# The last scatters of a part's rows moved from the attention stage's program into the expert stage's, in both layers of a two-layer transformer

## The reference

```python
x = layernorm(x + attention0(x))        # 16 heads of 8, 2048 tokens of 128, rotary, not causal
x = layernorm(x + moe0(x))              # 8 experts, top 2 of them, d_ff 384, and a shared expert of 128
x = layernorm(x + attention1(x))        # 8 heads of 128, causal, batches of 256 tokens
x = layernorm(x + block1(x))            # x + attn (16 heads of 8, causal, convolution in front), then x + moe1
# moe1: 4 experts, top 1, d_ff 512, no shared expert
#   h = layernorm(x) ; e = argmax(h @ router_w) ; y = (silu(h @ gate_e) * (h @ up_e)) @ down_e
```

## Time and profile before

| | |
|---|---|
| median of 3 runs | 1990.08 us (1985.74 to 1990.87) |
| the profiled execution | 1991.82 us, its span 1990.1 us |
| PE busy | 1785.9 us (90%) |
| DVE, ACT, POOL busy | 1562.2, 1375.0, 438.0 us |
| first layer's expert stage | from 703.4 us |
| second layer's expert stage | from 1891.3 us to the end |

### The profile page before, as it was taken

One profiled execution on the slowest core, in us unless ns is written; L12 is line 12 of the kernel. 1 busy time (PEld: TensorE's weight loads), 2 busy tenths in 40 slices (PEclk: granted clock), 3 DMA queues, 4 the chain that ended last, 5 costly groups with the idle time before them and its releaser, 6 DMA issues. The chain is left out here.

```text
span 1990.1 us, 40762 instructions
## 1 busy us (share of the span) xinstructions
PE 1785.9 (90%) x15944; PEld 978.8 (49%) x15944; DVE 1562.2 (78%) x2305; ACT 1375.0 (69%) x2571; POOL 438.0 (22%) x672
## 2 busy tenths in 40 slices
PE   6799999999999988858899999999679999999786
PEld 2122222222222368846789988989412322233386
DVE  5899999999999443456888888888578979786435
ACT  3499999999999843335566566666347898888432
POOL 4201000000000426323341221221320111122433
PEclk8589999999999988978999999999867999999688
DMA  6000000000000068700000000000100000000175
GB/s 175 1 3 4 4 11 3 3 12 3 4 12 5 20 228 271 258 28 1 1 1 1 1 1 1 1 1 1 56 1 2 5 3 12 5 12 6 44 247 199
DMA packets 50863, 82.01 MB, mean 41 GB/s; under 512 B 9424, under 2 KB 35280, under 8 KB 50544
## 3 DMA queue, kind: packets, MB, share of 16 engines
q1 hardware_dynamic: 44864, 69.53, 11.1%
q0 software_dynamic: 3712, 7.71, 1.1%
q10 hardware_dynamic: 2096, 2.17, 0.4%
HBM read 64.38 MB, written 12.25 MB: 39 GB/s over the span
## 5 line engine op out<-in xcount | busy, mean ns | idle before, releaser
L833 DVE TENSOR_REDUCE a_mx<-psum 128x2 f32<-128x1024 f32 (+2 forms) x832 | 906.4, 1159 | 76.5 <-PE psum L608 43.0
L759 ACT ACTIVATE a_cs<-psum 128x512 f32<-128x512 f32 (+3 forms) x1664 | 856.9, 571 | 80.9 <-PE psum L626 62.7
L649 PE MATMUL psum<-a_cs,a_V 128*16 128x256 f32 (+1 forms) x6400 | 501.7, 384 | 20.8 <-ACT a_OD L739 9.7
L608 PE MATMUL psum<-a_KS,a_QS 48*128 48x512 bf16 (+3 forms) x1664 | 329.9, 388 | 30.6 <-DVE a_mx L833 28.3
L626 PE MATMUL psum<-a_QS,a_KS 51*128 51x512 bf16 (+3 forms) x1664 | 336.8, 379 | 4.9 <-ACT a_cs L759 3.0
L626 PEld LDWEIGHTS psum<-a_QS,a_KS 51*128 51x128 bf16 x1664 | 87.8, 93 | 354.9 <-ACT a_cs L759 310.3
L2231 PEld LDWEIGHTS psum<-b_VW,b_ST 128*128 128x128 f32 x2176 | 247.4, 192 | 2.5 <-DVE X L2363 0.2
L2231 PE MATMUL psum<-b_VW,b_ST 128*128 128x129 f32 x2176 | 248.0, 275 | 0.0
L649 PEld LDWEIGHTS psum<-a_cs,a_V 128*16 128x16 f32 x6400 | 107.2, 94 | 245.1 <-issue 120.6
L2338 DVE TENSOR_TENSOR b_M<-b_M,b_ST 128x512 f32<-128x512 f32 (+3 forms) x264 | 158.0, 599 | 38.1 <-ACT b_ST L2270 7.8
L2270 ACT ACTIVATE b_ST<-psum 128x512 f32<-128x512 f32 (+1 forms) x320 | 149.9, 552 | 41.8 <-PE psum L2213 37.1
(11 more groups left out here) (250 smaller groups left out, 1839.6 us busy)
## 6 DMA issues: line engine op xcount, KB each, us to landing
e_W<-in_l_experts SPq DMA_DIRECT2D x45, 576.0 KB, 5.0
e_W<-in_l_experts SPq DMA_DIRECT2D x21, 768.0 KB, 6.0
e_G<-yg SPq DMA_DIRECT2D x12, 256.0 KB, 4.6
xg<-zeros SPq DMA_DIRECT2D x2, 1518.0 KB, 13.0
a_cs<-in_rope ACTq DMA_DIRECT2D x4, 512.0 KB, 10.1
a_QS<-a_mrow SPq DMA_DIRECT2D x128, 3.0 KB
a_cs<-in_rope SPq DMA_DIRECT2D x1, 2048.0 KB, 7.8
a_num<-a_OD SPq DMA_DIRECT2D x120, 16.0 KB
```

What stands on the lines that cost most here:

```text
L608: mm = pe.matmul(ps[:, 2 * slot + half, 0:width], QS[rows, 2 * p + i, q_cols(qb, qt * P, P)], KS[rows, 2 * p + i, c * BLK:c * BLK + width] ...
L649: mm = pe.matmul(ps[32 * j:32 * j + 2 * HD, AV_BANK, a:b], V[:, kt, HPP * p + j, :], probs(e, a, b), start=(kt == 0 and half == 0), stop=last,
L759: act.activation(probs(HPP * s + j, c, BLK), ps[:, plan.bank(entry), c:BLK], ACT.Exp, scale=scale).then_inc(exp_done, 1)
L833: dve.tensor_reduce(mx[:, pk % 2, qt, 2 * i:2 * i + 2, c], banks, AX.X, ALU.max).then_inc(max_done, 1)
```

## The change

`scatter` gets a range of tiles. The call at the end of the attention stage does the tiles before `AT_END`, and a new call in the expert stage, behind the powers of the late blocks and ahead of the first `give_back`, does the rest. `AT_END` is 5 in the first layer and 2 in the second. `sent[0]` is waited for as before.

```diff
@@ small_head_stage, gpsimd
                 for n in front.early:
                     front.keep_early(pool, n)
-                front.scatter(pool, 0)
+                front.scatter(pool, 0, 0, front.AT_END)
@@ Front.__init__
+            self.AT_END = 5
         else:
...
+            self.AT_END = 2
@@ Front
-    def scatter(self, pool, b):
+    def scatter(self, pool, b, first=0, last=None):
         pool.wait_ge(self.pos_ready, b + 1)
         if b == 0:
             pool.wait_ge(self.half_set, 2)
             pool.wait_ge(*self.blank)
-        for t in self.plan.tiles[b]:
+        for t in self.plan.tiles[b][first:last]:
             for k in range(self.K):
@@ expert_layer, gpsimd
                 following.begin(pool)
                 for n in front.late:
                     front.power(pool, n)
+                front.scatter(pool, 0, front.AT_END)
```

## The result

The changed kernel takes 2000.34 us (median of 5 runs, 1998.93 to 2003.88), the kernel before 1990.08 us (5 runs, 1984.48 to 1990.87). The ratio over all runs is 1.0064, with a 95% interval of 1.0045 to 1.0084, so the change costs 0.64%, about 12.7 us (8.9 to 16.7). This ratio is not the quotient of the two medians, which differ by 10.3 us. It is slower, as forecast, but the forecast was 19.8 us and its range began at 2003.5. The profiled execution took 2000.34 us with a span of 1998.6 us.

What follows compares the result with a forecast made beforehand. Both borders were taken to wait for POOL's scatters, with PE the chain behind. First layer 5.0 plus second 14.8, the borders' gain included, gave 19.8 us on 1990.1: 2010 us, range 2003.5 to 2015.5.

Steps and rivals of the forecast that it cites:

- the order of what is queued behind the scatters: SP's weight loads for tiles 1 to 5 stand behind the row loads; on PE everything behind `turn(0)` waits in order.
- the mechanism in both layers: Expert stages: moved scatters make SP issue rows 14.6 us later; PE waits at `turn(0)` in the second, tile 1 in the first.
- a second part that takes nothing back: Tile 1's delay reaches each stage's end in full, since later row waits (4.32, 4.87 us) are timed by scatters following tiles.
- clock term: First layer, tiles 1 and 2 after PE's wait: the lower clock makes five steps take 6.85 us instead of 5.50, 1.35 more.
- lock between DVE and POOL: DVE's normalizing groups beside moved scatters: at most 0.2 us per layer, left out; the skill's rule would add some 2 us.
- The step that failed: the border: Both borders before the expert stages come 0.78 and 1.89 us earlier, 2.67 us in all, with DVE next in line.
- the weights in the first layer: First layer, tile 1: weights queued behind rows start it 10.5 us after the row issue, +3.7 us (+1.7 to +4.2).
- The term of the first layer: First layer's expert stage: late weights at tile 1, +3.7 us, and lower clock, 1.35 us; sum +5.0 us (1.7 to 5.6).
- The second layer's term: Second layer's expert stage: late rows hold PE 15 us at `turn(0)`, tile 1 14.6 us late, 0.2 for clock; +14.8 us.
- (a): First layer: weights come in time because DMA engines were idle, tile 1 loses nothing; sum +13.8, 2004 us; chance 0.10.
- (b): Both layers: the lower clock lasts longer after PE stands, or DVE blocks scatters about a microsecond; 2014.5 us; chance 0.12.
- (c): Expert stage hides the six scatters completely, only the borders' gain is left: 1987.4 us; chance 0.01.

## Why the prediction was wrong in size

**Right.** What bounds the borders, that the gain there is small against the loss, the order of what is queued behind the scatters, and the mechanism in both layers: rows 15.6 and 16.5 us into the stages (15.4 and 16.5 forecast), PE standing 14.95 us in the second (15), 3.63 us at tile 1 in the first (3 to 5), a second part that takes nothing back, and a clock term of 6.92 - 5.50 = 1.42 us (1.35). No lock between DVE and POOL of a size that matters: the first moved scatter of the second layer took 1.03 us, the others 0.96, and they came every 1.26 to 1.34 us. In the first layer DVE's group of four normalizing instructions beside the first scatter took 1.14 us, and 1.11 without a scatter beside it (scatters ahead of the powers).

**The step that failed: the border.** I took the gain as the gap between the two last arrivals, 0.78 and 1.89 us, "with the same delay from the last arrival to the start of the next stage as now (2.27 and 1.96 us)". That delay does not belong to the border but, for its greater part, to POOL when scatters are its last work. With DVE last it is 0.28 us. The gains are 2.80 and 3.57 us: 2.0 and 1.7 more than forecast, 3.7 of the 7.1 us by which the sum was too large (19.8 against 12.7). The rows of the draining line in the trace of before had it. The prediction went by the idle time ahead of POOL's first instruction alone, whose releaser was named as POOL's own sequencer.

**The second term that was mis-sized: the weights in the first layer.** I took tile 1 at 10.5 us behind the row issue, by the second part's 11.0, within bounds of 8.5 and 11.0. It was 9.00 (and 9.00 in the run of the first layer alone). This is 1.5 us. Neither distance is a constant. The second part's 11.0 is one end of a spread: it was 9.5 to 9.7 in five other traces and 11.0 to 11.1 in three. And in two traces with the first layer as before the first weights landed 9.6 and 10.1 us behind the row issue. The term of the first layer then is 5.0 - 2.0 - 1.5 + 0.2 (the rows' own 0.24) + 0.1 (clock) = 1.8 us. Measured: 1.86 us at the transpose behind tile 2, and +1.7 us (-0.2 to +3.6) for the layer alone by its runs. That these three agree so closely is luck, since the clock alone moves the trace's number by 1.5 us from one execution of before's program to the next.

**The second layer's term.** 14.8 less 1.7 for the border and 0.4 for the weights (tile 1 at 7.86 us behind the row issue, not 8.26) is 12.7. The 0.4 may be chance: in the other traces with late rows the distance is 7.99 to 8.26 us. In the trace tile 1 loses 12.5, and the stage to its end 15.3 - 3.6 = 11.7; the runs of the layer alone say +11.7. The 0.8 us between 12.5 and 11.7 is within what the stage's length varies by among traces of one program, so it isn't shown that anything was taken back behind tile 1.

**The sum again.** 1.8 + 11.7 to 12.7 is 13.5 to 14.5 us, by the two layers' runs 13.4, and the change as measured is 12.7 (8.9 to 16.7 by its interval). What is left over is within the measurement. The terms that were off come to 5.6 of the 7.1 us, with the doubtful 0.4 in it.

**The rivals.** (a), weights in time in the first layer, did not happen, though its 2004 was nearer than the forecast: its price of tile 1 was wrong and the time came down for another reason. The experiment with the loads reversed shows what it would have taken. (b), more for the clock or the port, found no support: in the first layer the low clock cost 1.42 us as in the forecast, and the second layer's tile 1 ran in 2.05 us. (c) was excluded rightly for the whole change, and its mechanism is what makes the kernel with two scatters moved in the first layer faster than before. (d) is excluded: the second part's wait was 4.98 us after 4.87.

**The range.** Its lower end was made from bounds of the weights alone. The border had no bound of its own, because I took the delay behind the last arrival for a constant. One bound, that the delay might be POOL's, would have lowered that end by 3.7 us, to 1999.8.

## What to carry to other kernels

When work is taken off the engine that arrives last at a border, the gain is not the gap between the last arrivals: read the end of each engine's drain at that line, since the delay behind the last instruction differs by engine and by what it did last. In these traces the next stage began 0.2 to 0.6 us behind the last drain's end. When a transfer is made later, cost the whole queue behind it; here the weights behind the rows, not the rows, were the first layer's loss, and issuing them first removed it. When a single trace is set against another, look at the clock of the stretch first. Move only as much as the next stage has cover for: two scatters into a stage with 17 us of other work ahead of the rows gained 3.4 us, six into one with 4 us lost 11.7.

## What the runs showed of the hardware

POOL's drain ended 2.0 and 1.7 us behind the end of its last indirect DMA in the trace of before, and in the traces with scatters last on POOL the next stage started 1.95 to 2.6 us behind the end of that DMA. With DVE last it started 0.28 us behind, and with powers last on POOL, in one execution, 1.44 and 0.47 us. The landing of that DMA is not the whole of it: a scatter of this kernel lands 2.27 us after its start, which is 1.3 us after its end, and the drain ends up to 0.7 us after that. The drain is not the whole of it either. With 14 scatters ahead of the border, POOL's drain ended at 699.86 and DVE's at 699.7, and the stage began at 700.37. What the 0.5 us are stays open.

In the changed kernel the first load of weights behind the rows (576 KB) landed in 6.6 us. The rows ahead of it in the queue are 1518 KB, and in these 6.6 us the DMA engines moved 342 GB/s, with the profile's DMA share at 1.12, so they were fully taken. In the kernel with `AT_END` 5 and the weights first, the same load was issued with nothing ahead of it. SP, and the landing of the first of the five:

```profile
700.10 4.77 SPq L1317 DMA_DIRECT2D e_W<-in_l_experts  x5
...
DMA to landing us min/median/max: 3.4/3.4/3.4
```

The second landed in 5.7 us and the third in 6.1, with the loads ahead of them still under way. The Trainium skill, "DMA: Bandwidth & Descriptors", section "Anatomy of one DMA — SWDGE (gpsimd) path", gives its fit for DMAs issued by POOL; the estimate by it for a load of this size, which SP issues here, is 3.4 us, as the prediction said. The trace agrees for the load with nothing ahead of it, and not for the one behind the rows, where the measured 6.6 decides. So the engines that rival (a) found idle are no longer idle once the rows stand ahead of the weights.

PE came back from standing 15 us at a granted clock of 0.50 (1904 to 1908): `up(0)` took 3.62 us, where the same 16 records take 1.95 later, and the next tile, at 0.91 (1908 to 1911), was at nearly full speed (2.05 us). In the first layer the tile after 3.63 us of standing was slow and so was part of the next (2.90, then 2.23 us; 1.50 later). Tile 1 was at the lower clock there before too, so only the second of these is new. The stop of 15 us cost no more clock than the one of 4. But the clock also fell where PE had stood for a microsecond at most. In the first layer, where neither rows nor weights were waited for, tiles 0 and 1 took 2.77 and 2.77 us before, 2.63 and 1.50 with the second layer's change alone, 2.57 and 2.02 with `AT_END` 5 and the weights first, and 1.51 and 1.50 with 14 scatters ahead of the border.
